# First layer's output stage: gated values in a place of their own for each group, masks one group ahead of additions, and two more gates moved ahead

## What is computed

```python
# L0_conv: from h = layernorm(x) come gated products x1, x2 (8 channels each)
t = jnp.concatenate([x1, x2], axis=-1)              # 16 channels a token
t = _layernorm(t, ln2_w, ln2_b)                     # over the 16 channels
po_out = t @ po_w + po_b                            # 16 -> 32 channels
go_logits = t @ go_w + go_b
return po_out * jax.nn.sigmoid(go_logits) * mask[..., None]
# in the caller
x = x + _L0_conv_ref(_ln_c(x), ...)
t = _to_tokens(x)
t = t + _L0_ffn_ref(_ln_t(t), ...)                  # layernorm of x, batchnorm, recurrence
```

## Time and profile before

| | |
|---|---|
| median of 3 executions | 311.65 us (309.08 to 313.02) |
| profiled execution | 310.83 us, of which the span of the core is 309.1 us |
| PE busy | 239.2 us (77%) |
| DVE busy | 229.0 us (74%) |
| POOL busy | 155.1 us (50%) |
| ACT busy | 116.6 us (38%) |
| chain that ended last, by engine | PE 43%, DVE 35%, POOL 7%, issue 6%, ACT 6% |
| granted TensorE clock over the span | 0.887 of full |

### The profile page before, as it was taken

How to read it: one execution, slowest core, us unless ns; L and a number is a source line. 1 busy time by engine, 2 the same in 40 slices (tenths; PEclk the granted TensorE clock), 3 DMA queues, 4 the chain that set the end, 5 groups by cost and what they waited for, 6 DMA issues and landing times.

```text
span 309.1 us, 4512 instructions
## 1 busy us (share of the span) xinstructions
PE 239.2 (77%) x1509; PEld 169.3 (55%) x1509; DVE 229.0 (74%) x406; ACT 116.6 (38%) x226; POOL 155.1 (50%) x209
## 2 busy tenths in 40 slices
PE   0298986947279989997969999886146999889894
PEld 0176776434134468995756859885146972333331
DVE  4998555987887620388884556989999998798893
ACT  4342434225324145544544637752321250221310
POOL 4405473059900059530619979954933528866100
PEclk9999988796859999999999999999655555999998
DMA  6200000000000000000000000000008961958401
GB/s 219 68 14 1 0 3 0 0 2 1 0 0 0 3 0 0 0 2 2 0 4 0 2 0 0 2 0 2 0 0 202 206 141 34 206 158 186 130 36 68
DMA packets 6635, 13.08 MB, mean 42 GB/s; under 512 B 2774, under 2 KB 3030, under 8 KB 6614
## 3 DMA queue, kind: packets, MB, share of 16 engines
q1 hardware_dynamic: 6470, 12.81, 16.2%
q10 hardware_dynamic: 144, 0.01, 0.0%
HBM read 2.32 MB, written 2.10 MB: 14 GB/s over the span
## 4 chain that ended last, share of the span: by engine, by line
PE 43%; DVE 35%; POOL 7%; issue 6%; ACT 6%; DMA 2%; SPq 0%; POOLq 0%; DVEq 0%; ACTq 0%
PE ps L1412 5%; PE ps L995 4%; PE ps L991 4%; DVE var L370 4%; PE ps L1391 3%; PE ps L1067 3%; DVE sums L332 3%; POOL x L806 3%; POOL gated L789 2%; PE ps L1297 2%; PE ps L1282 2%; PE ps L606 2%; PE ps L1112 2%; DVE gated L1905 2%; PE ps L1404 2%
## 5 line engine op out<-in xcount | busy, mean ns | idle before, releaser
L606 PE MATMUL ps<-ident,xn 128*128 128x128 f32 x144 | 28.3, 332 | 16.7 <-DVE xn L595 8.0
L606 PEld LDWEIGHTS ps<-ident,xn 128*128 128x128 f32 x144 | 20.0, 172 | 29.1 <-issue 9.1
L806 POOL TENSOR_TENSOR x<-x,sg 128x512 f32 x16 | 22.0, 1389 | 9.1 <-DVE sg L1958 7.6
L1905 DVE TENSOR_TENSOR gated<-ps,sg 128x512 f32 (+1 forms) x16 | 16.6, 1048 | 10.7 <-ACT sg L1570 10.1
L1067 PE MATMUL ps<-ones_b,ones_h 128*128 128x512 bf16 x50 | 16.2, 479 | 10.4 <-ACT v_wrap L1519 7.5
L1028 ACT ACTIVATE gated_t<-ps,bn 128x128 f32<-128x128 f32 x54 | 16.9, 364 | 13.8 <-PE ps L995 13.0
L789 POOL TENSOR_TENSOR gated<-gated,mask_e 128x512 f32<-128x512 f32 x16 | 20.3, 1322 | 2.0 <-DVE gated L1905 2.0
L789 POOL TENSOR_TENSOR gated<-gated,mask_a x8 | 11.4, 1428 | 18.6 <-DVE gated L1731 18.6
L1391 PE MATMUL ps<-gated,pick 96*128 96x512 bf16 x64 | 20.3, 428 | 0.1
L370 DVE TENSOR_REDUCE var<-squares 128x32 f32<-128x1024 f32 (+1 forms) x18 | 19.6, 1091 | 0.8 <-POOL squares L347 0.8
L615 ACT ACTIVATE xt<-ps 128x512 f32<-128x512 f32 (+1 forms) x24 | 12.2, 524 | 16.9 <-PE ps L606 12.0
(11 more groups left out here) (279 smaller groups left out, 650.3 us busy)
## 6 DMA issues: line engine op xcount, KB each, us to landing
out_gate<-gated SPq DMA_DIRECT2D x32, 128.0 KB, 2.3
x<-gated SPq DMA_DIRECT2D x32, 128.0 KB, 2.4
x<-in_x_dram SPq DMA_DIRECT2D x4, 512.0 KB, 5.7
out_dram<-x SPq DMA_DIRECT2D x8, 256.0 KB, 2.0
e_full<-in_L_ffn_expert_b_dram SPq DMA_DIRECT2D x12, 1.0 KB
mask_a<-in_L_conv_mask_dram SPq DMA_DIRECT2D x1, 64.0 KB, 6.4
mask_c<-in_L_conv_mask_dram SPq DMA_DIRECT2D x1, 64.0 KB, 1.8
w_x<-in_L_ffn_expert_w_dram SPq DMA_DIRECT2D x1, 32.0 KB
```

The lines of the kernel that those rows point to most:

```text
L606: ins = pe.transpose(bank(s)[:, t * P:(t + 1) * P], xn[:, s, t, :], ident[:, :])
L806: pool.tensor_tensor(v, v, sg[:, s, :], ALU.add).then_inc(pj.added, 1)
L1905: dve.tensor_tensor(o, v, sg[:, h, :].rearrange("p (u s o) -> p u s o", u=2, s=S), ALU.mult).then_inc(p_c.used, 1)
```

## The change

It has four parts, all in this stage. `gate_o` writes its result to `out_of(g)`, a place of its own for each group in the tensor `gated`, whose earlier contents are used up; `sg` holds only the sigmoids, and `gates_o` on ACT waits until the gate two groups back has been taken (`used`), not until its addition is done (`added`). POOL masks group 0, then runs seven times through "mask of group g+1, addition of group g", then makes the last addition. On DVE the gate of group 1 moves ahead of the second chain and the gate of group 2 into its middle. After the chain each `scale(g)` is followed by `gate(g-1)`, where it was followed by `gate(g-2)`.

```diff
+        def out_of(g):
+            v = gated[:, 0:C, :].rearrange("p (g a) b -> p g (a b)", a=GROUP)
+            return v[:, bass.ds(g, 1), :].rearrange("p a n -> p (a n)")
...
             chain(dve, dve.scalar_tensor_tensor(t, t, -10.0 / 3, t, ALU.add, ALU.mult), step)
+            if midway:
+                midway()
             chain(dve, dve.scalar_tensor_tensor(y, t, 5.0, y, ALU.add, ALU.mult), step)
...
+        def fused_dve_o(dve, ready, scale, gate, after):
...
+            take_spread(dve, n_o, 1)
+            gate(0, 0, True)
+            scale(3, 1, False)
+            gate(1, 1, False)
+            take_rstd(dve, n_o, 1, midway=lambda: gate(2, 0, False))
+            dve.wait_ge(n_o.done, 2)
+            for g in range(4, GROUPS + 1):
+                if g < GROUPS:
+                    scale(g, g % 2, False)
+                gate(g - 1, (g - 1) % 2, False)
+                if g - 1 in after:
+                    after[g - 1]()
...
-            def mask_and_add(g, s, early):
+            def mask_o(g):
                 pool.wait_ge(p_o.used, g + 1)
...
+            def add_o(g):
                 pool.wait_ge(p_o.masked, g + 1)
...
+                pool.tensor_tensor(v, v, out_of(g), ALU.add).then_inc(p_o.added, 1)
+
+            mask_o(0)
+            with pool.Fori(0, GROUPS - 1) as g:
+                mask_o(g + 1)
+                add_o(g)
+            add_o(GROUPS - 1)
...
                 act.wait_ge(p_o.projected, g + 1)
                 if not early:
-                    act.wait_ge(p_o.added, g - 1)
+                    act.wait_ge(p_o.used, g - 1)
...
-                dve.tensor_tensor(w, v, w, ALU.mult).then_inc(p_o.used, 1)
+                o = out_of(g).rearrange("p (t r n) -> p r t n", t=2, r=2)
+                dve.tensor_tensor(o, v, w, ALU.mult).then_inc(p_o.used, 1)
```

More of the change, by code:

```diff
@@ L383, in take_var, with root_of @@
             take_rstd(dve, nm, p)
-        def root_of(dve, v, y, t, step=dve_step):
+        def root_of(dve, v, y, t, step=dve_step, midway=None):
             chain(dve, dve.tensor_scalar(y.bitcast(I32), v.bitcast(I32), -0.5, ROOT, ALU.mult, ALU.add), step)
@@ L393, in root_of, with take_rstd @@
             chain(dve, dve.scalar_tensor_tensor(t, t, -0.5 * CUBIC ** 3, v, ALU.mult, ALU.mult), step)
-        def take_rstd(dve, nm, p, step=dve_step, done=None):
+        def take_rstd(dve, nm, p, step=dve_step, done=None, midway=None):
             v, y, t = piece(nm, sd, p), piece(nm, rstd, p), piece(nm, newton, p)
-            root_of(dve, v, y, t, step)
+            root_of(dve, v, y, t, step, midway)
             dve.scalar_tensor_tensor(y, t, 1.5 * CUBIC, y, ALU.add, ALU.mult).then_inc(done or nm.done, 1)
@@ L444, in fused_dve, with reduce @@
             gate(GROUPS - 1, 1, False)
+        def fused_dve_o(dve, ready, scale, gate, after):
+            def reduce(q):
+                take_sum(dve, n_o, pair_t, q, ready)
+                chain(dve, take_squares(dve, n_o, q))
+            take_sum(dve, n_o, pair_t, 0, ready)
+            take_squares(dve, n_o, 0)
+            take_sum(dve, n_o, pair_t, 1, ready)
+            chain(dve, take_squares(dve, n_o, 1))
+            take_var(dve, n_o, 0)
+            dve.wait_ge(n_o.done, 1)
+            scale(0, 0, True)
+            scale(1, 1, True)
+            reduce(2)
+            scale(2, 0, False)
+            reduce(3)
+            take_spread(dve, n_o, 1)
[10 more added lines that the diff above has]
+                    after[g - 1]()
         def fused_pool(pool, nm, work):
@@ L807, in add_out @@
                 return f
-            def mask_and_add(g, s, early):
+            def mask_o(g):
                 pool.wait_ge(p_o.used, g + 1)
                 m = mask_a[:, :].rearrange("p (g t) -> p g t", t=16)[:, bass.ds(g, 1), :]
-                v = sg[:, s, :].rearrange("p (t o) -> p t o", o=C)
+                v = out_of(g).rearrange("p (t o) -> p t o", o=C)
                 pool.tensor_tensor(v, v, bcast(m.rearrange("p a t -> p (a t)"), C),
                                    ALU.mult).then_inc(p_o.masked, 1)
+            def add_o(g):
                 pool.wait_ge(p_o.masked, g + 1)
[L816 to L820, removed]
+                v = x[:, :, :].rearrange("p (g t) c -> p g (t c)", t=16)[:, bass.ds(g, 1), :]
+                v = v.rearrange("p a n -> p (a n)")
+                pool.tensor_tensor(v, v, out_of(g), ALU.add).then_inc(p_o.added, 1)
[4 more added lines that the diff above has]
+            add_o(GROUPS - 1)
             pool.wait_ge(bn_dve, 4)
@@ L1775, in whole_b @@
                 return take_squares(dve, n_b, q)
-            fused_dve(dve, n_o, pair_t, pair_ready, scale_group(dve, p_o, D2, prod), gate_o,
+            fused_dve_o(dve, pair_ready, scale_group(dve, p_o, D2, prod), gate_o,
                       after={3: lambda: take_sum(dve, n_b, x, 0, x_added),
```

## The result

The changed kernel takes **318.86 us** (median of 4 executions, 318.01 to 322.24) against 310.48 us (4 executions) for the kernel before, measured beside it: a ratio of **1.028**, 95% interval 1.023 to 1.033. It is slower by 8.4 us; forecast were 321.0 us and a chance of 0.80 for slower. The profiled execution took 319.31 us.

The account below looks back on a forecast made before the run. POOL's masks and additions, ending at 85.22 us, were taken as the bound. Gate 3 at 70.35 + 3 x 5.87 + 6.65 = 94.6 us, 9.4 later, gave a median of 321.0 us, range 316 to 323.3.

Parts of the forecast that it names:

- What bounds the stage: End of the stage: POOL's last addition ends at 85.22 us, and the last quarter's sum and everything behind it follow.
- Masks ahead: 2.24 us a group, where POOL has work: POOL: each addition finds its mask done, so a group costs 2.24 us instead of 2.46, at most 1.8 us saved.
- Two gates forward: DVE's second chain: mask 1 starts at 64.06, one chain operation passes per POOL instruction, gate 3 starts at 70.35.
- The ring: Gates 3 to 6: each gate waits through PE and ACT for the scale directly ahead; closed rounds of 5.87 us.
- Which clock: TensorE pauses in the new rounds, so all three run at the lower clock: 5.87 us each, not 4.58.
- From gate 6 to the end: POOL: 0.88 us to gate 6's mask, then 5.75 without a gap; last addition ends 6.65 after gate 6 starts.
- The sum: Whole stage: 70.35 + 3 x 5.87 + 6.65 = 94.6 us against 85.22, so it ends 9.4 us later.
- I add nothing for the rest.: Program behind the stage: it moves along with the last addition, no other stage changes, so zero is added.
- the rival with the clock up in one or two rounds: Rounds from gate 3 to 6: one or two at the higher clock, 318.5 to 319.7 us; chance 0.15.
- POOL stays the bound, and the change gains: Masks and additions: with rounds of at most 2.24 us POOL ends at 81.0, 4.2 earlier, 307.4 us; chance 0.03.

Follow-up runs that it names:

- experiment 8: Changed kernel with the second chain ahead of gate 0, each scale three gates ahead, ACT's squares later: 308.64 us, ratio 0.996 to the kernel before.
- experiment 1: Changed kernel with DVE's order put back to that of the kernel before, masks ahead and own places kept: 312.44 us, ratio 1.003 to the kernel before.
- experiment 2: Kernel before with only the new DVE order, shared buffers and old POOL order kept: 320.11 us, ratio 1.032 to the kernel before.
- experiment 3: Changed kernel with each scale from group 5 on moved one gate earlier, two gates ahead again: 312.31 us, ratio 1.005 to the kernel before.
- experiment 9: Changed kernel with DVE's and POOL's old orders, leaving only own places and ACT's shorter wait: 310.09 us, ratio 0.999 to the kernel before.
- 5: Changed kernel with PE projecting a group ahead of the next one's transposes from group 4 on: 316.20 us, ratio 1.021 to the kernel before.
- 4: Changed kernel with POOL's order put back to mask, then addition, group by group: 319.13 us, ratio 1.030 to the kernel before.
- 10: As experiment 8, but POOL takes mask, then addition, group by group: 309.76 us, ratio 0.997 to the kernel before.
- 11: Kernel before with only experiment 8's order on DVE and ACT, old shared buffers and POOL order kept: 310.54 us, ratio 0.999 to the kernel before.
- experiments 6: Changed kernel with PE's order turned from group 4 on and ACT's sigmoid ahead of the next group's copy: 315.47 us, ratio 1.019 to the kernel before.

## Why the prediction was right

The forecast was 321.0 us with a range of 316.0 to 323.3; it came out at 318.86. Step by step:

- *What bounds the stage.* Right. The last addition ends the stage in every version, and what follows starts on it.
- *Masks ahead: 2.24 us a group, where POOL has work.* Right in size (2.23 in experiment 8, where no `scale` stretches POOL), and right that POOL has no work here. Not foreseen was the price beside it: the sums wait for a later addition, 1.7 us of stage under the old order.
- *Two gates forward.* The steps landed within 0.2 us: mask 1 directly behind mask 0 (forecast 64.06 to 65.11; the pair of masks runs from 62.82 to 65.01), mask 2 at 67.58 (67.6), gate 3 at 70.31 (70.35). One chain operation per POOL instruction held in all five cases.
- *The ring.* Right, and the whole of the loss (experiments 1, 2 and 3). Rounds of 5.95, 5.97 and 5.53 against 3 x 5.87, in sum 17.45 against 17.61. The term is 0.08 to 0.10 short in the first two: I took 0.47 for `scale` beside a mask, and without POOL's gap it took 0.56.
- *Which clock.* Right for what TensorE does in two rounds, and a step wrong in "Nothing that I read shows the clock rising in such a pattern": it did rise, at 81 to 82 us. It fell again at 85 to 86, before most of the third round's products, so that this gained only 0.44 us (5.97 against 5.53).
- *From gate 6 to the end.* 6.69 against 6.65 (the terms written there add up to 6.63).
- *The sum.* Last addition at 94.45 against 94.6. Shift of the stage 9.23 against 9.4.
- *"I add nothing for the rest."* Here the profile differs from the sum. The shift stays at 9.2 to 9.5 us until late in the program, and then about 1 us is given back in the last stage. The rows, of the kernel before and then of the one after:

```profile
266.41 0.42 DVE L2055 TENSOR_REDUCE red<-gated_t 128x32 f32<-128x256 f32 x1 [0.27 <-POOL gated_t L954]
...
285.78 1.22 DVE L2038 TENSOR_TENSOR squares<-ps,out_gate 128x1024 f32<-128x1024 f32 x1
```

```profile
275.86 0.42 DVE L2099 TENSOR_REDUCE red<-gated_t 128x32 f32<-128x256 f32 x1 [1.72 <-POOL gated_t L997]
...
294.26 1.22 DVE L2082 TENSOR_TENSOR squares<-ps,out_gate 128x1024 f32<-128x1024 f32 x1
```

And the clock there, after:

```profile
268.00:270.00 2.00, 2.00 (x11) 0.34 (x13) 2.00 (x3) 0.00 (x0) 1.85 (x3) 0.63 0.00 0
270.00:272.00 2.00, 1.81 (x16) 0.44 (x9) 1.61 (x3) 0.86 (x3) 1.83 (x4) 1.00 0.53 119
```

The first pair is 9.45 us apart, the second 8.48. After, the clock is back at 1.00 by 270 us. The same work in the kernel before, 9.4 us earlier, would be at 260.6, and there the window 260 to 262 read 0.50 and 262 to 264 read 0.71. So the clock came back some 3 us earlier in the work. It does not follow the shift. Take the span less the start of the last quarter's sums, which is all that lies behind the stage: it is 223.85 us before and 223.12 after, but also 223.06 in experiment 9, whose stage is that of before, and 223.03 in 5, while 4, moved nearly as far as the changed kernel, has 223.84. In these three short ones the clock rose about 175 us behind the start of those sums; in the other ten it rose about 176 to 178.5 us behind it, and the rest is 223.8 to 224.4 us. So 0.7 us of the difference goes with when the clock rises in one execution, whatever the order in this stage, and zero for the rest of the program stands. What decides when it rises was not tested.

The difference between 321.0 and 318.86 is then this. The profiled execution came out 0.9 below its forecast of 320.2: 0.2 in the stage and 0.7 behind it. The other 1.25 is the median, which I had put 0.8 above the profiled execution, from three executions; the medians lie 0.35 and 0.45 below them. So 318.86 lies in the band of the rival with the clock up in one or two rounds (318.5 to 319.7) by chance: of the 1.29 us that a full round at the higher clock gives, 0.44 came.

The rival "POOL stays the bound, and the change gains" had its turning point right: it needs rounds at POOL's own pace, which experiment 8 reaches by another order. It then gains 1.2 us and not 4.2, because the second chain has to be done first.

## What to carry to other kernels

When a step is moved on an in-order engine, count how many steps lie between an input's production and its use once round the whole ring of engines, not on that engine alone: here three `scale` steps, each one gate too late, cost 8 us, and moving them back returned nearly all of it. Work one group ahead on the last engine paid here where everything before it is early (1.0 us of stage gained in experiment 8 against 10), and cost where it is not (1.7 us in experiment 1 against 9, 0.6 in the changed kernel against 4). And if something is to be moved earlier into a chain of small operations, look first at what these run beside: moving the chain itself did better here, though it won only 0.4% over the kernel before, and nothing without the masks ahead (experiments 10 and 11, not told from before).

## What the runs showed of the hardware

- A small DVE operation with SBUF inputs beside a POOL instruction takes until about the end of that instruction: 0.97 to 1.20 us instead of 0.23 (0.44 to 0.81 where it starts in the middle of it). Between two POOL instructions without a gap one such operation passes, and in POOL's gap of 0.16 to 0.20 us another passes in 0.23. This holds in every version in which the chain runs beside POOL.
- The collision works back. A `scale` of 0.42 us that meets POOL instructions without a gap takes 0.56, and the addition behind the mask 1.45 instead of 1.27. With POOL's gap of 0.16 us between mask and addition they took 0.49 and 1.27 (experiment 4). In experiments 6 and 1 a `scale` that met an addition took 1.43 and 1.34.
- A wait for the instruction directly ahead costs POOL a gap of 0.16 to 0.20 us. When the wait is met one instruction earlier, the next instruction starts 0.04 before the end of the row ahead. That is 0.2 us a group, and 1.0 us of stage over the eight groups between experiments 8 and 10, in which DVE's collisions are counted in.
- The granted clock also differed ahead of the stage: from 45 to 50 us it was 1.00 in experiments 5, 8, 9 and 10, where the stage began 1.4 to 2.1 us early, 0.69 before and 0.74 after. What decides that from one execution to the next stays open.
- About the same work of TensorE (2.9 us without a pause, twice) brought the granted clock up behind the second round of the changed kernel and not behind the first, and it fell again 4 us later (81 to 86 us). When it rises in the last stage also differs between profiled executions, by 3 to 4 us, and the three in which it rose first are the three that are 0.7 us shorter there.
